# Attention and soft mixture of experts on one core: x transposed loaded and split before the key and value weights, slot embeddings scaled by GpSimd and transposed by PE, value sums moved, logits kept with a constant

## What is computed

```
x = x + layernorm(attention(layernorm(x)))
x = x + layernorm(soft_moe(layernorm(x)))

attention: q, k, v = x w_qkv (16 heads of 16)
           dots = q k^T;  attn = dots / max(|dots| per row, 1e-12) * norm_g + norm_b
           out = (attn v) w_out + b_out
soft_moe:  xn = rmsnorm(x, gamma);  sn = rmsnorm(slot_embeds, slot_gamma)
           logits[n, e, s] = xn . sn
           dispatch = softmax over n;  combine = softmax over (e, s)
           slots = dispatch^T xn;  expert e: gelu(slots w1 + b1) w2 + b2
           out = combine . experts
```

## Time and profile before

| | us |
|---|---|
| median of three runs | 821.07 |
| lowest and highest | 820.95, 821.4 |
| the profiled execution | 820.74 |
| its span, first to last instruction | 818.9 |
| the attention stage, PE, start of batch 0's gram to the first logits | 8 to 150 |
| PE busy | 807.9 (99%) |
| DVE busy | 699.0 (85%) |
| ACT busy | 630.4 (77%) |
| POOL busy | 168.4 (21%) |

### The profile page before, as it was taken

How to read it: one execution, slowest core, us unless ns; L and a number is a source line. 1 busy time by engine, 2 the same in 40 slices (tenths; PEclk the granted TensorE clock), 3 DMA queues, 4 the chain that set the end, 5 groups by cost and what they waited for, 6 DMA issues and landing times.

```text
span 818.9 us, 16585 instructions
## 1 busy us (share of the span) xinstructions
PE 807.9 (99%) x5186; PEld 718.8 (88%) x5186; DVE 699.0 (85%) x1373; ACT 630.4 (77%) x1269; POOL 168.4 (21%) x211
## 2 busy tenths in 40 slices
PE   8999999999999999999999999999999999999997
PEld 7888888888888888887998999999999999999997
DVE  8798988799999989998958888888888889487776
ACT  5676766667786886789668888988888888777775
POOL 0100000033223333552420414141413122000000
PEclk9999999999999999999999999999999999999999
DMA  8322230102323253225102011020202020376893
GB/s 295 132 78 78 78 126 28 52 26 91 104 91 126 81 205 103 78 80 172 58 1 83 22 46 58 21 81 4 99 0 102 0 102 0 102 245 199 280 296 112
DMA packets 55011, 80.63 MB, mean 98 GB/s; under 512 B 3248, under 2 KB 33840, under 8 KB 54832
## 3 DMA queue, kind: packets, MB, share of 16 engines
q1 hardware_dynamic: 54960, 80.00, 29.0%
HBM read 54.83 MB, written 25.17 MB: 98 GB/s over the span
## 4 chain that ended last, share of the span: by engine, by line
PE 85%; DVE 5%; ACT 2%; issue 2%; POOL 0%; ACTq 0%; DVEq 0%; POOLq 0%
PE bank L1138 22%; PE bank L1182 17%; PE bank L1247 11%; PE bank L1025 9%; PE bank L1000 8%; PE bank L1130 3%; PE bank L1009 2%; PE bank L931 2%; PE bank L884 2%; PE bank L904 1%; PE bank L914 1%; PE bank L894 1%; PE bank L821 1%; PE bank L843 1%; PE bank L990 1%
## 5 line engine op out<-in xcount | busy, mean ns | idle before, releaser
L1138 PEld LDWEIGHTS bank<-w_r,act_r 128*128 128x128 f32 x1536 | 199.2, 190 | 11.3 <-issue 1.0
L1138 PE MATMUL bank<-w_r,act_r 128*128 128x256 f32 x1536 | 202.7, 282 | 0.0
L1025 PE MATMUL bank<-disp_r,y_r 128*128 128x512 f32 x384 | 103.4, 406 | 0.6 <-DVE disp_r L2297 0.4
L1000 PE MATMUL bank<-yT_r,snT 128*128 128x512 f32 x384 | 100.3, 397 | 0.0
L2509 DVE TENSOR_TENSOR act_r<-act,act_r 128x512 fp32r<-128x512 f32 x112 | 82.4, 742 | 18.8 <-ACT act_r L1708 18.7
L1247 PE MATMUL bank<-eo_r,comb_r 128*128 128x258 f32 x768 | 92.1, 282 | 0.0
L1247 PEld LDWEIGHTS bank<-eo_r,comb_r 128*128 128x128 f32 x768 | 92.0, 189 | 0.0
L1182 PE MATMUL bank<-snT,w_op 128*128 128x512 f32 x336 | 87.7, 395 | 0.2 <-DVE act L2503 0.2
L1000 PEld LDWEIGHTS bank<-yT_r,snT 128*128 128x128 f32 x384 | 71.6, 188 | 16.4 <-issue 0.5
L1025 PEld LDWEIGHTS bank<-disp_r,y_r 128*128 128x128 f32 x384 | 67.7, 189 | 13.3 <-DVE disp_r L2297 1.0
L1708 ACT ACTIVATE act_r<-act 128x512 fp32r<-128x512 f32 x112 | 70.9, 633 | 10.1
(11 more groups left out here) (235 smaller groups left out, 1637.1 us busy)
## 6 DMA issues: line engine op xcount, KB each, us to landing
combine_scratch<-comb SPq DMA_DIRECT2D x64, 256.0 KB, 2.0
stage<-in_w SPq DMA_DIRECT2D x16, 1024.0 KB, 5.5
stage<-combine_scratch SPq DMA_DIRECT2D x4, 2048.0 KB, 9.1
snT<-combine_scratch SPq DMA_DIRECT2D x4, 2048.0 KB, 9.4
slots_eo<-in_x_t SPq DMA_DIRECT2D x8, 512.0 KB, 6.1
x_scratch<-stage SPq DMA_DIRECT2D x8, 512.0 KB, 3.2
x<-x_scratch SPq DMA_DIRECT2D x8, 512.0 KB, 4.4
x_d<-x_scratch SPq DMA_DIRECT2D x8, 512.0 KB, 9.7
```

Source lines behind the costliest of these rows:

```text
L1000: last = pe.matmul(bank[m % 2][:, :], snT[:, i, k, m * S:(m + 1) * S], yT_r[:, j, k, :], start=(n == 0), stop=(n == len(steps) - 1))
L1025: last = pe.matmul(bank[4 + k][:, :], y_r[:, i, t, k * P:(k + 1) * P], disp_r[h][:, j, t, :], start=(n == 0), stop=(n == len(fill_steps) - 1))
L1138: done = pe.matmul(bank[BH + 2 * f + c // 2][:, (c % 2) * D:(c % 2 + 1) * D], act_r[:, tile, a, c * S:(c + 1) * S], w2_r[:, w, j, :], star ...
```

## The change

- **SP** loads, behind the first x, the query weights, then x transposed of batch 0, then the key and value weights, then the identity. Before, the identity came first and x transposed last. The load of `seT` is gone.
- **ACT and DVE** round and split in stage 0 in the order x transposed, query weights, key and value weights. Before: key and value weights, query weights, x transposed.
- **POOL** copies the statistics and the floor of every batch (`keep_stats`), which DVE did. Between batches 1 and 2 it scales `se` by `se_scale`, eight pieces of 128x256.
- **PE** transposes the scaled `se` behind the stages 1 and 2, eight 128x128 blocks each (`transpose_slots`), into banks 4 and 5. ACT and DVE round and split `snT` from there. `gram_times_q` of the next stage waits for it.
- **PE** makes the value sums of an odd stage between the outputs and the norms, into free columns of bank 3. They wait for the new `xsum_kept`; the copy `vb` then stands behind the clamp on DVE, and gram times k of an odd stage waits for it.
- **DVE** normalises half of the next x before the remainder of `gk_r` and half behind it; the two head copies of L2061 are one instruction; `keep_logits` multiplies by −1 instead of by the column.
- Some semaphores are merged. The math is the same.

Two of the four normalisations moved behind the remainder of gk_r, the copies went to POOL, and vb moved up behind the clamp. The core of the diff:

```diff
@@ sync
-            sp.dma_start(ident[:], identity).then_inc(ident_loaded, 16)
             sp.dma_start(wqkvT[:, :, 0:D], wqkv_v[:, :, 0:D]).then_inc(wq_loaded, 16)
+            sp.dma_start(xT[:, 0], xt_v[:, 0:KD, :]).then_inc(xT_loaded[0], 16)
             sp.dma_start(wqkvT[:, :, D:3 * D], wqkv_v[:, :, D:3 * D]).then_inc(wkv_loaded, 16)
-            sp.dma_start(xT[:, 0], xt_v[:, 0:KD, :]).then_inc(xT_loaded[0], 16)
+            sp.dma_start(ident[:], identity).then_inc(ident_loaded, 16)
...
-            sp.dma_start(seT, slots_t.rearrange("(k p) n -> p k n", p=P)).then_inc(se_loaded, 16)
@@ gpsimd
+            def keep_stats(b):
+                pool.wait_ge(x_aggr, b + 1)
...
+                nc.gpsimd.tensor_copy(mv_x[:, ds(b * NT, NT), :], mv[:])
+                nc.gpsimd.tensor_scalar(norm_floor[:, ds(b * NT, NT)], mv[:, :, 1], LN_EPS, NORM_EPS * NORM_EPS,
+                                        ALU.add, ALU.mult).then_inc(x_mean_kept, 1)
...
+            pool.wait_ge(se_step, 4)
+            for h in range(HALVES):
+                for n in range(h * EH, (h + 1) * EH):
+                    last = nc.gpsimd.tensor_scalar(se[:, n, :], se[:, n, :], se_scale[:, n:n + 1], 1.0,
+                                                   ALU.mult, ALU.mult)
+                last.then_inc(se_normed, 1)
@@ tensor
             def gram_times_k
...
+                    if odd:
+                        pe.wait_ge(vb_kept, sums_through(b, True, it))
             def value_sums(b):
...
-                pe.wait_ge(qT_ready, b * KD + 1)
+                where, at = sums_at(b)
+                if is_batch(b, 0):
+                    pe.wait_ge(qT_ready, 1)
+                else:
+                    pe.wait_ge(xsum_kept, b + 1)
             def gram_times_q
...
+                    pe.wait_ge(snT_ready, KD if second else KD * HALVES)
+            def transpose_slots(h):
+
+                pe.wait_ge(se_normed, h + 1)
+                pe.wait_ge(oT_split, h + 1)
+                for k in range(KD):
+                    for e in range(EH):
+                        last = pe.transpose(bank[4 + k][:, e * S:(e + 1) * S],
+                                            se[:, h * EH + e, k * P:(k + 1) * P], ident[:])
+                    last.then_inc(seT_in_psum, 1)
             attention(1, True, first_back=True)
+            transpose_slots(0)
             attention(2, False, second_back=True)
+            transpose_slots(1)
@@ scalar
             def round_slots(h):
...
-                    act_fn(snT[:, 0, k, cols], seT[:, k, cols], ACT.Copy, scale=both_gam[:, k:k + 1])\
+                    sc.wait_ge(seT_in_psum, h * KD + k + 1)
+                    act_fn(snT[:, 0, k, h * EH * S:(h + 1) * EH * S], bank[4 + k][:, :], ACT.Copy,
@@ vector
             def stats_of_x
...
+                dve.wait_ge(x_mean_kept, b)
             def keep_sums
...
+                if not is_batch(b, 0):
+                    dve.wait_ge(norm_in_psum, b)
             def keep_logits
...
-                v.tensor_scalar(neg_logits(b, m), bank[m % 2][:, :], se_scale[:, m:m + 1], None, ALU.mult, ALU.min,
+                v.tensor_scalar(neg_logits(b, m), bank[m % 2][:, :], -1.0, None, ALU.mult, ALU.min,
```

More of the change, by code:

```diff
@@ L708, in _ @@
                     .then_inc(wout_centred, 1)
-            pool.wait_ge(bout_summed, 1)
-            nc.gpsimd.tensor_scalar(bout_bc[:], bout_bc[:], b_mean[:], None, ALU.subtract).then_inc(bout_centred, 1)
+            pool.wait_ge(wout_summed, KD + 1)
+            nc.gpsimd.tensor_scalar(bout_bc[:], bout_bc[:], b_mean[:], None, ALU.subtract).then_inc(wout_centred, 1)
+            pool.wait_ge(se_step, 4)
[4 more added lines that the diff above has]
+                last.then_inc(se_normed, 1)
+            for b in range(2, B):
+                keep_stats(b)
             def normalise_dispatch(b, m):
@@ L861, in value_sums @@
                 pair = slice(b, b + 1) if is_batch(b, 0) or is_batch(b, 1) else slice(0, 2)
-                pe.wait_ge(qT_ready, b * KD + 1)
+                where, at = sums_at(b)
+                if is_batch(b, 0):
+                    pe.wait_ge(qT_ready, 1)
+                else:
+                    pe.wait_ge(xsum_kept, b + 1)
                 for h in range(KD):
                     for k in range(KD):
-                        last = pe.matmul(bank[0][:, 2 * h + pair.start:2 * h + pair.stop],
+                        last = pe.matmul(where[:, at + 2 * h + pair.start:at + 2 * h + pair.stop],
                                          wqkvT[:, k, 2 * D + h * P:2 * D + (h + 1) * P], xsum[:, pair, k],
@@ L871, in queries @@
                 pe.wait_ge(xT_split, b + 1)
-                pe.wait_ge(wqkv_split, 2)
+                pe.wait_ge(wqkv_split, 1)
                 if is_batch(b, 1):
                     pe.wait_ge(vb_kept, 1)
-                elif not odd and not is_batch(b, 0):
-                    pe.wait_ge(vb_kept, sums_through(b - 1, True, it))
                 if symmetric(b):
@@ L945, in attention @@
                     outputs(b - 1, first_back)
+                    if odd:
+                        value_sums(b)
                     norms(b - 1)
                 queries(b, odd, it, [0])
-                gram_times_k(b)
+                gram_times_k(b, odd, it)
                 queries(b, odd, it, [1])
-                if odd or not back:
+                if not back:
                     value_sums(b)
@@ L1349, in keep_xsum @@
                     alone(sc)
-                    act_fn(xsum[:, u], gram[:, :, D:D + 1].rearrange("p k a -> p (k a)"), ACT.Copy)
+                    last = act_fn(xsum[:, u], gram[:, :, D:D + 1].rearrange("p k a -> p (k a)"), ACT.Copy)
                 else:
@@ L1353, in keep_xsum @@
                     for m in range(KD):
-                        act_fn(xsum[:, u, m:m + 1], gram_bank(b, m)[:, D:D + 1], ACT.Copy)
+                        last = act_fn(xsum[:, u, m:m + 1], gram_bank(b, m)[:, D:D + 1], ACT.Copy)
+                last.then_inc(xsum_kept, 1)
             def round_gram(b, first):
@@ L1918, in rest_of_slots @@
                     cols = slice(h * EH * S, (h + 1) * EH * S)
-                    v.scalar_tensor_tensor(out=snT[:, 1, k, cols], in0=seT[:, k, cols],
+                    v.scalar_tensor_tensor(out=snT[:, 1, k, cols], in0=bank[4 + k][:, :],
                                            scalar=both_gam[:, k:k + 1], in1=snT[:, 0, k, cols].bitcast(F32),
@@ L2175, in attention @@
                     clamp_norm(b - 1)
+                if odd:
+                    keep_sums(b, it)
+                if back:
                     scale_o(b - 1)
@@ L2189, in attention @@
                     rest_of_gk(b)
-                if front and not back:
-                    norm_x(1, NT // 2, NT)
+                if following:
+                    norm_x(b + 1, NT // 2, NT)
                 if back:
```

70 lines of the change are left out of this document (33 added, 37 removed).

## The result

| | before | after |
|---|---|---|
| median | 820.95 (5 runs) | 826.36 (5 runs) |
| lowest and highest | 820.62, 821.4 | 825.17, 828.17 |
| the profiled execution | 820.74 | 826.77 |
| its span | 818.9 | 825.0 |
| mean granted clock of PE in its span | 1.000 | 0.993 |

The ratio is 1.0061, with a 95% interval of 1.0045 to 1.0076: the changed kernel is slower, and by more than the prediction's range allowed. The forecast was 822.1.

The account below looks back on a forecast made before the run. PE, busy 99% of the span at full clock, was taken as the bound. Terms −0.6 − 0.3 + 1.7 + 0.2 = +1.0 on 820.74 gave 821.7, plus 0.33 for the median 822.1; own range 821.3 to 823.3, wider range 820.4 to 823.8.

Parts of the forecast that it names:

- Batch 1 and the order inside a batch: Value sums moved before norms, normalisation halved: batch 1 gains 0.3, transposes to projection 3.03; loop batches 0; bounds 0 and 0.6.
- Start, −0.6: Batch 0, x transposed split before the weights: gram times Wk 0.8 earlier, of which 0.6 taken; bounds 0.2 and 0.8.
- Slots, +1.7: Sixteen slot transposes on PE behind the projections of batches 1 and 2, 0.85 per eight: +1.7, bounds 1.6 and 2.1.
- new constant in the logits' copy: The −1 constant in the logits' copy: taken as 0, with a gain of up to 1.3 as far bound.
- doubt about GpSimd: GpSimd's slot scaling may slow VectorE's L2145 on batch 1's path: 0 to +0.9, taken as 0.
- Value sums against xsum, +0.2: Odd batches' value sums now wait for xsum, written behind ScalarE's four squares: +0.2, bounds 0 and +0.6.
- The loop's waits go after all: Rival: G·Wk and head products hold the projection, so batches 2 to 6 gain 0.65 each, time 818.9; chance 0.12.
- The slots come late: Rival: the slots' rounding ends late and delays PE in batches 2 and 3, 1.0 each: +3.0, 824.1; chance 0.15.
- The start gives nothing: Rival: x transposed lands late or batch 1's start hangs on something else: +1.6, 822.7; chance 0.10.
- transposes one after another: Rival: sixteen slot transposes run in series at 272 ns, 4.4 instead of 1.7: +3.7, 824.8; chance 0.05.

Follow-up runs that it names:

- experiment 1: The changed kernel with the value sums of the odd stages, and their copy vb, back behind the queries: 822.38, ratio 1.0015.
- experiment with `vb` late: Two runs took vb behind the remainder of G·Wk: the changed kernel with value sums back, 821.59; the kernel before with start's order and halved normalisation, 819.74.
- experiment 1 with `vb` late: The changed kernel with the value sums back behind the queries and vb behind the remainder of G·Wk: 821.59.
- last run of experiment 7: The kernel before with the start's order, the halved normalisation and vb behind the remainder of G·Wk: 819.74, ratio 0.9982.

## Why the prediction was wrong

**The step that failed** stands in *Batch 1 and the order inside a batch*: moving the value sums was put at nothing, since their number is the same. PE's own work is the same indeed. But the clock at which PE does it isn't, and there was no term for it. The earlier trace rows had the clock at full speed in all slices of before, and I took that for a property of the kernel instead of one of this order of work. Their new place costs 4 us (experiment 1 against the changed kernel), more than the whole range.

**Start, −0.6.** Right: queries at 11.15 as forecast 11.1, gram times Wk at 12.86 against 13.0, batch 1's gram at 18.95 against 19.0, which is −0.7. The start alone gave −0.5 in the median.

**Batch 1, −0.3.** Wrong. The wait on G·Wk is gone, yet from the transposes to the projection batch 1 takes 37.12 − 33.87 = 3.25, where it took 3.28, and not 3.03. VectorE was ready: the first of its two subtractions waited 0.78 for ScalarE's rounding, which starts 1.0 behind the transposes. In batch 6 it started 0.78 behind them, and that is most of the 0.25 between 3.28 and 3.03. The wait that I removed covered another of the same length, as the experiment with `vb` late shows too (3.28 with no wait on gk_r). The gain was 0.

**Slots, +1.7.** Right, with some luck. PE goes on 40.85 − 40.06 = 0.79 behind each group of eight transposes, and the path costs 1.8. But two things that the prediction put at nothing offset each other. The stages 2 and 3 lost 0.2 and 0.5 more: from gram to gram they take 19.30, of which 0.79 is transposes, and 19.24 in experiment 1 with `vb` late, against 18.33 and 18.75 in the last run of experiment 7, which has no slots' path. And behind the first transpose of y the executions with the slots' path took 674.4 to 674.7, those without it 674.7 to 675.1. That shorter end is the only sign of the new constant in the logits' copy; no run has the constant without the rest of the slots' path. The forecast's doubt about GpSimd was right in kind. In the changed kernel two pieces of the normalisation take 1.13 beside its scaling and 0.73 elsewhere:

```profile
15.21 0.74 DVE L2042 TENSOR_SCALAR xn<-slots_eo,mv,rstd 128x256 f32<-128x256 f32 x2
...
31.34 1.13 DVE L2042 TENSOR_SCALAR xn<-slots_eo,mv,rstd 128x256 f32<-128x256 f32 x2
31.35 4.31 POOL L728 TENSOR_SCALAR slots_eo<-slots_eo,se_scale 128x256 f32<-128x256 f32 x8 [4.16 <-DVE se_scale L1953]
...
33.97 0.90 DVE L2042 TENSOR_SCALAR xn<-slots_eo,mv,rstd 128x256 f32<-128x256 f32 x2
```

The instruction that I had named, the remainder of the output weights, took 0.67 there, as before, and 0.83 in experiment 1. The Trainium skill (GPSIMD Engine Reference, 1. Specifications) says that GpSimd's SBUF interfaces are shared with VectorE, with contention for VectorE instructions in a 2-port mode or with two SBUF inputs. The trace agrees with the sharing, by the normalisation pieces; for the one with two SBUF inputs, the named instruction, the traces are divided. The 0.57 that it cost in the normalisation lay beside ScalarE's rounding and was nobody's wait.

**Value sums against xsum, +0.2.** Not seen. xsum is ready at 66.17 + 0.19 = 66.36, and PE starts the value sums of stage 3 at 66.41, close behind. But that is 66.41 − 64.48 = 1.93 after the outputs' start, and the norms of the kernel before came 63.45 − 61.52 = 1.93 after theirs. In stage 5 the distance is 1.79 in both. So the new wait cost nothing in this execution.

**The rivals.** *The loop's waits go after all*: it fell, 3.03 between transposes and projection in stages 2, 4 and 6 as before. (The prediction took 0.65 a batch for that wait; its own rows give 3.03 − 2.30 = 0.73.) *The slots come late*: the first split ended at 42.82, a microsecond before gram times q at 43.80; the second cost 0.1. *The start gives nothing* and *transposes one after another* fell by the numbers above. Three of the four were about waits and one about the pitch of transposes. None was about the clock of PE, so none could have given 826. Without the falls the sum was good: experiment 1, which has none, stands 0.3 above the forecast, with 0.6 of loss of its own by `vb`. That it was this good is in part luck, since the terms of batch 1, of xsum, of the logits' copy and of the slots were off by 0.2 to 0.7, in different directions.

## What to carry to other kernels

Moving matmuls within an engine that hardly waits isn't free by itself: the place can decide at which clock the next ones run. Look at the clock of each run, not only of one profile, and at the granted clock in stretches of 2 us, since the page's 40 slices hide a fall that costs 1.5. If two groups of identical matmuls in one stage differ by a factor near two with no wait between them, as 2.91 and 1.56 did here, look at the clock first.

## What the runs showed of the hardware that I had not expected

The granted clock of a PE that is 98 to 99% busy fell from 2.4 to 1.2 GHz for about 3 us, in the first queries and gram times k of an odd stage, at 1.5 to 1.7 us each. It differed from run to run: 0 to 3 falls in the profiled executions, and by its mean clock the kernel before has them too, in 13 of 92 runs. The changed kernel's windows ahead of its first and its second fall:

```profile
22.00:28.00 6.00, 6.00 (x45) 5.04 (x43) 2.50 (x9) 3.96 (x17) 0.92 (x1) 0.99 0.88 309
60.50:69.30 8.80, 8.80 (x63) 7.50 (x63) 8.26 (x21) 6.22 (x20) 0.39 (x2) 0.98 0.00 0
```

PE has no gap in them, and the clock is at 0.98 to 0.99, falling only at their very end. DMA traffic alone doesn't explain the fall: its share was 0.88 in one and 0.00 in the other. The Trainium skill (TensorE: Matmul & The Clock Gate, Part 1, HAM oscillation and the section behind it, on cycling through PSUM banks) describes falls of the clock where PE waits for data, or idles briefly between groups of matmuls. No idle time stands in these rows, so they don't show either case. The ends of matmuls are modelled, though, and their records overlap, so a full row doesn't prove that PE was fully used. What in the products, sums and norms lets the clock fall stays open. Narrowness of the added work isn't needed, a piece of queries between them doesn't help, and whether the stretch begins before gram times q wasn't settled.
